# Expert outputs added by GpSimd for 32 of 64 row tiles, by VectorE for the rest; four buffers for the rows that feed layer 1's gates

## What is computed

```python
x  = L0_attn_x
xn = layernorm(x)
x  = x + L0_attn(xn) + L0_moe(xn)     # 16 heads of 8, attention between the heads of one row
xn = layernorm(x)
x  = x + L1_attn(xn) + L1_moe(xn)     # two gated causal convolutions over time

def moe(xn):                          # 8 experts, hidden size 512, two experts per row
    top_w, top_i = top2(xn @ W_gate)
    return sum(weight * (gelu(xn @ W_in[e] + b_in[e]) @ W_out[e] + b_out[e]) for the two experts e)
```

## Time and profile before

| | us |
|---|---|
| median of 3 runs | 1330.55 (1329.0 to 1339.67) |
| the profiled execution | 1335.22 |
| its span, first to last instruction | 1333.3 |
| busy: PE / DVE / ACT / POOL | 1042.1 / 739.9 / 583.7 / 803.9 |

### The profile page before, as it was taken

The page is one execution under the profiler, slowest core; times in us unless marked ns, Lnnn a source line. Parts: engine busy times, 40 slices in busy tenths (PEclk is TensorE's granted clock), DMA queues, the critical chain, the costliest instruction groups (busy, mean ns, idle before and its releaser), DMA issues. The chain is left out here.

```text
span 1333.3 us, 19064 instructions
## 1 busy us (share of the span) xinstructions
PE 1042.1 (78%) x6498; PEld 879.2 (66%) x6498; DVE 739.9 (55%) x953; ACT 583.7 (44%) x1518; POOL 803.9 (60%) x669
## 2 busy tenths in 40 slices
PE   5553776788988898888714678898879999999995
PEld 4521333367777777777613577888868888888884
DVE  7755988998888898888697643211122200000007
ACT  1200111166676777767503673000006666666651
POOL 4065675568888888888875136566544544444444
PEclk9876886799999999999856888998979999999998
DMA  9912322335554555555281021698966867666649
GB/s 294 355 47 102 120 84 109 108 93 151 155 162 139 154 170 149 161 150 159 68 325 57 1 84 44 197 279 252 296 196 195 270 193 196 194 190 196 199 135 356
DMA packets 120245, 226.03 MB, mean 170 GB/s; under 512 B 16961, under 2 KB 80405, under 8 KB 118102
## 3 DMA queue, kind: packets, MB, share of 16 engines
q1 hardware_dynamic: 102164, 188.45, 46.1%
q0 software_dynamic: 17600, 35.71, 7.3%
q10 hardware_dynamic: 386, 0.66, 0.2%
HBM read 157.33 MB, written 67.42 MB: 169 GB/s over the span
## 5 line engine op out<-in xcount | busy, mean ns | idle before, releaser
L498 POOL DMA_INDIRECT y_tok<-FF,yidx x284 | 283.3, 997 | 205.9 <-ACT FF L586 142.6
L490 POOL DMA_INDIRECT sorted_x<-XN,idx x256 | 247.9, 968 | 140.1 <-issue 88.0
L810 PE MATMUL ps<-FF 128*128 128x128 f32 x2272 | 285.8, 280 | 0.0
L810 PEld LDWEIGHTS ps<-FF 128*128 128x128 f32 x2272 | 274.0, 197 | 15.6 <-issue 4.8
L797 PE MATMUL ps<-FF 128*128 128x256 f32 x1136 | 272.3, 383 | 0.0
L576 ACT ACTIVATE FF<-ps,FF 128x256 f32<-128x256 f32 x568 | 231.4, 473 | 36.8 <-PE ps L797 29.1
L797 PEld LDWEIGHTS ps<-FF 128*128 128x128 f32 x1136 | 206.9, 192 | 22.7
L294 POOL TENSOR_TENSOR BG<-TPB 128x2048 f32<-128x2048 f32 x42 | 188.8, 4519 | 30.0 <-ACT TPB L603 20.8
L838 PE MATMUL ps<-BG,cst 128*128 128x512 f32 x176 | 105.4, 767 | 57.8 <-DVE BG L1144 40.5
L1176 DVE TENSOR_TENSOR BG<-ps,TPB 128x1024 f32<-128x1024 f32 x128 | 147.3, 1212 | 0.0
L1187 DVE TENSOR_REDUCE BG<-BG 128x256 f32<-128x4096 f32 x32 | 141.0, 4406 | 0.0
(11 more groups left out here) (203 smaller groups left out, 1462.0 us busy)
## 6 DMA issues: line engine op xcount, KB each, us to landing
FF<-in_moe SPq DMA_DIRECT2D x142, 514.0 KB
TPB<-in_kpad SPq DMA_DIRECT2D x22, 1024.0 KB
sorted_x<-TPB SPq DMA_DIRECT2D x36, 520.0 KB, 5.4
FF<-sorted_x SPq DMA_DIRECT2D x142, 130.0 KB
BG<-y_tok SPq DMA_DIRECT2D x12, 1024.0 KB, 9.2
FF<-in_kpad SPq DMA_DIRECT2D x10, 1024.0 KB
y_tok<-FF,yidx POOLq DMA_INDIRECT x284
xt_d<-BG SPq DMA_DIRECT2D x16, 256.0 KB, 4.4
```

The lines of the kernel that those rows point to most:

```text
L490: pool.indirect_dma_start(sorted_x[layer], bass.IndirectOffsetOnAxis(ap=idx[:, k, j:j + 1], axis=0), XN[:, j, :], None).then_inc(s_sc, 16)
L498: pool.indirect_dma_start(y_d[layer], bass.IndirectOffsetOnAxis(ap=yidx[:, G % 4, r:r + 1], axis=0), ys[:, G % 4, r * D:(r + 1) * D], None ...
L810: t = pe.matmul(psY[:, r * P:(r + 1) * P], hT[:, G % 2, m, r * P:(r + 1) * P], wc[:, G % 4, HID + m * D:HID + (m + 1) * D], start=False, s ...
```

## The change

Four things are altered. (1) Between the layers POOL adds only pieces 0 to 3 (`ADD_POOL = 4`), adding the two outputs to `X` one after the other; pieces 4 to 7 are added by DVE with the same two instructions inside rounds 2 and 3, ahead of their statistics. (2) POOL's `wait_ge(s_comb, 8)` ahead of its normalised rows goes. (3) The gate rows have four buffers, two of `xg` and two of `xT`, so that an engine waits for the transposes of four groups before instead of two; and DVE makes the rows of groups 1, 3, 5, 7, 11 and 15 only, ACT all others, so groups 9 and 13 move from DVE to ACT. (4) At the end DVE adds both outputs of all eight pieces, and POOL none.

```diff
-            def add_outputs(layer, i):
-                pool.wait_ge(s_yl[i], 16 * (layer + 1))
-                y = outputs(layer, i)
-                return pool.tensor_tensor(y[:, :, 0:D], y[:, :, 0:D], y[:, :, D:2 * D], ALU.add)
-
-            for i in range(8):
-                plink(add_outputs(0, i))
+            for i in range(ADD_POOL):
+                pool.wait_ge(s_yl[i], 16)
                 pool.wait_ge(s_xup, 4 * i + 4)
-                xv = X[:, 8 * i:8 * i + 8, :]
-                pool.tensor_tensor(xv, xv, outputs(0, i)[:, :, 0:D], ALU.add).then_inc(s_comb, 1)
-            pool.wait_ge(s_comb, 8)
+                y, xv = outputs(0, i), X[:, 8 * i:8 * i + 8, :]
+                plink(pool.tensor_tensor(xv, xv, y[:, :, D:2 * D], ALU.add))
+                pool.tensor_tensor(xv, xv, y[:, :, 0:D], ALU.add).then_inc(s_comb, 1)
...
-            for i in range(1, 7):
-                add_outputs(1, i).then_inc(s_ysum, 1)
...
+        def by_dve(g):
+            return g % 4 == 3 or g % 4 == 1 and g < NG // 2
+        def gate_rows(g):
+            return (xg, xT)[g % 2][:, (g // 2) % 2, :]
...
-                for g in (4 * q, 4 * q + 2):
-                    wait(act, s_tr, NG + g - 1 if g >= 2 else 0)
-                    for k in range(4):
-                        t = norm_rows(xg[:, 0, k * D:(k + 1) * D], 4 * g + k, 1)
-                    t.then_inc(s_hg[0], 1)
+                for g in range(4 * q, 4 * q + 4):
+                    if not by_dve(g):
+                        wait(act, s_tr, NG + g - 3 if g >= 4 else 0)
+                        for k in range(4):
+                            t = norm_rows(gate_rows(g)[:, k * D:(k + 1) * D], 4 * g + k, 1)
+                        t.then_inc(s_hg, 1)
...
-            def combine(i):
-                y = outputs(1, i)
-                rv = R[:, 8 * i:8 * i + 8, :]
-                if 1 <= i < 7:
-                    dve.wait_ge(s_ysum, i)
-                else:
-                    dve.wait_ge(s_yl[i], 32)
-                    link(dve.tensor_tensor(rv, rv, y[:, :, D:2 * D], ALU.add))
-                dve.tensor_tensor(rv, rv, y[:, :, 0:D], ALU.add).then_inc(s_comb, 1)
-                dve.wait_ge(s_comb, 8 + i + 1)
+            def combine(layer, dst, i):
+                dve.wait_ge(s_yl[i], 16 * (layer + 1))
+                y = outputs(layer, i)
+                dv = dst[:, 8 * i:8 * i + 8, :]
+                link(dve.tensor_tensor(dv, dv, y[:, :, D:2 * D], ALU.add))
+                dve.tensor_tensor(dv, dv, y[:, :, 0:D], ALU.add).then_inc(s_comb, 1)
+                dve.wait_ge(s_comb, 8 * layer + i + 1)
...
             for q in range(4):
-                dve.wait_ge(s_comb, 2 * q + 2)
+                for i in (2 * q, 2 * q + 1):
+                    if i < ADD_POOL:
+                        dve.wait_ge(s_comb, i + 1)
+                    else:
+                        combine(0, X, i)
                 stats_of(X, 16 * q, 16 * q + 16)
```

More of the change, by code:

```diff
@@ L52 @@
 ROWS_PARTS = 7
+ADD_POOL = 4
 COUNTS_AT = 7
@@ L246, in mixed_layers @@
         s_comb = sem("combined")
-        s_ysum = sem("expert_outputs_summed")
         s_resst = sem("x1_stored")
         s_resld = sem("x1_loaded")
-        s_hg = [sem(f"gate_rows{n}") for n in range(2)]
+        s_hg = sem("gate_rows_of_scalar")
+        s_hd = sem("gate_rows_of_vector")
         s_xnr = sem("layer1_rows_ready")
@@ L765, in transposes_and_gates @@
                         bank = psH[g % 4]
-                        pe.wait_ge(s_hg[g % 2], g // 2 + 1)
+                        made = len([n for n in range(g + 1) if by_dve(n) == by_dve(g)])
+                        pe.wait_ge(s_hd if by_dve(g) else s_hg, made)
                         wait(pe, s_xt, NG + g - 3 if g >= 4 else 0)
                     for k in range(4):
-                        src = XN[:, 4 * g + k, 0:D] if layer == 0 else xg[:, g % 2, k * D:(k + 1) * D]
+                        src = XN[:, 4 * g + k, 0:D] if layer == 0 else gate_rows(g)[:, k * D:(k + 1) * D]
                         t = pe.transpose(bank[:, k * P:(k + 1) * P], src, ident)
@@ L1265, in _ @@
                 for g in (4 * q + 1, 4 * q + 3):
-                    wait(dve, s_tr, NG + g - 1 if g >= 2 else 0)
-                    for j in range(4 * g, 4 * g + 4):
-                        t = dve.tensor_scalar(xg[:, 1, (j - 4 * g) * D:(j - 4 * g + 1) * D], X[:, j, :], rstd[:, 1, j:j + 1],
-                                              shift[:, 1, j:j + 1], ALU.mult, ALU.add)
-                    t.then_inc(s_hg[1], 1)
+                    if by_dve(g):
+                        wait(dve, s_tr, NG + g - 3 if g >= 4 else 0)
+                        for k in range(4):
+                            j = 4 * g + k
+                            t = dve.tensor_scalar(gate_rows(g)[:, k * D:(k + 1) * D], X[:, j, :], rstd[:, 1, j:j + 1],
+                                                  shift[:, 1, j:j + 1], ALU.mult, ALU.add)
+                        t.then_inc(s_hd, 1)
             ratio = best[:, 5, :]
@@ L1289, in _ @@
             dve.wait_ge(s_xnr, ROWS_PARTS)
-            for n in range(2):
-                dve.wait_ge(s_hg[n], NG // 2)
+            dve.wait_ge(s_tr, 2 * NG)
             dve.wait_ge(s_resst, 16 * 8)
@@ L1326, in _ @@
                 dve.wait_ge(s_oev, 2 * i + 2)
-                combine(i)
+                combine(1, R, i)
                 for g in (2 * i + 4, 2 * i + 5):
```

## The result

The changed kernel takes 1317.74 us (median of 20 runs, 1310.82 to 1324.09), the one before 1329.40 in 20 runs beside them (1321.49 to 1339.67): a ratio of 0.9912, 95% interval 0.9894 to 0.9931, or 11.7 us less (9.2 to 14.1). The forecast was 10.7 us less. The profiled execution took 1315.85 us, its span is 1314.0 us. Against the profiled execution of before (1335.22) that is 19.4 us, more than the medians show, so the first question is which part of the 19.4 belongs to the change.

A forecast was written before the change was run, and what follows sets the result against it. Between the layers all wait for DVE's first shift, its short products held by POOL's adds. Terms -11.8 + 2.4 - 0.5 - 0.8 = -10.7 us, from the median 1330.55 to 1320; range 1311 to 1329.

The forecast's parts named there:

- The stalls of round 0: Between the layers: without POOL's adds of pieces 4 to 7, DVE's first shift comes 11.8 us earlier.
- the other 1.5 us: DVE's product at 694.49, before round 0's statistics, would take 0.42 us without POOL beside it instead of 1.93.
- The rounds: Rounds 1 to 3 with DVE's adds: 8.9, 13.1, 12.0 and 2.0 contention, together 36.0 us, 2.4 more than before.
- the contention: Rounds 2 and 3: DVE's eight adds lose 2.0 us to POOL's normalised rows; bounds 0 and 3.4.
- Last shift to routing: Gate rows of groups 9 and 13 on ACT: routing begins 0.5 us sooner after the last shift; bounds 1.2 less, 1.0 more.
- The end: End of the kernel, DVE adding alone: pieces 3.73 us each, 27.4 us in all, 0.8 less; bounds 0 and 1.6 less.
- The first, over 1% faster: DVE's adds hardly meet POOL and ACT's square root is not late: 13.6 us less, 1317; chance 0.24.
- The second, a loss after 758 us: After routing, one more wait like ACT's 8.17 us takes the gain to 2.5 us: 1328; chance 0.08.
- The third, adds at 3.29 us: DVE's eight adds become the bound at 3.29 us each: 3.5 us slower, 1334; chance 0.04.
- The fourth, a round 1 of 10.8 us: Four buffers fail, ACT and PE keep round 1 at 10.8 us: 1322; chance within the forecast's 0.64.

The follow-up runs named there:

- e3: Kernel before, with POOL's adds of pieces 4 to 7 started only after the first shift; ratio 1.0011 to the kernel before.
- e1: Changed kernel, but POOL adds all eight pieces to `X` between the layers; ratio 0.9944 to the kernel before.
- e9: Changed kernel; POOL adds pieces 0 to 2, sums outputs of pieces 3 to 6 beside statistics, normalised rows after fourth shift; 1312.46 us.
- e5: Changed kernel; POOL sums the outputs of pieces 4 and 6 beside DVE's statistics, its normalised rows after the fourth shift; ratio 0.9894 to the kernel before.
- e7: Changed kernel, with POOL's normalised rows all started after the fourth shift; ratio 0.9888 to the kernel before.

## Why the prediction was right, and where a term was mis-sized

**The stalls of round 0 (-11.8).** Measured -11.45, and the short products at 0.17 us. The 10.3 us inside round 0 came out at 10.4 (16.64 to 6.25). The mis-sized part is the other 1.5 us, which did not show where the prediction put them: the product before the statistics took 1.93 us again, at 690.01, since DVE came to it 4.5 us earlier than in the trace that was read (694.49) while POOL's eighth add ended at about the same time (694.15; 693.85 before), so it ran beside piece 3 instead of piece 4. It took 1.93 to 1.95 in all seven profiles in which POOL makes these eight adds and then stops or waits. Another product gave 1.05 instead (2.04 at 682.43 before, 0.99 at 679.00 after). That is luck: the same product took 0.85 in e3, where POOL's adds up to there are those of the kernel before. In the trace of three pieces, where POOL was through in time, the product before the statistics took 0.42, as priced. The assumption that failed is that POOL's last kept add ends ahead of that product, as it did in the one trace that was read.

**The rounds (+2.4).** Measured +1.0 (34.60 against 33.59). Round 1, put at 8.9, took 8.77, and DVE's idle time of 1.07 for the square root was in it as predicted. For rounds 2 and 3 the instructions were put at 13.1 and 12.0, and without POOL beside them they took 13.06 and 12.03. The mis-sized term is the contention: "60% of 0.46 for eight adds is 2.2. I take 2.0" is 0.7 as measured. The 60% came from DVE's adds beside POOL's adds of 2.35 us, where DVE gives way; beside POOL's rows of 0.46 us POOL gave way, about 4 us in each round, and was not on the path. From the rule of the Trainium skill, SBUF — State Buffer, section Who interferes with whom, the prediction had worked out a saving of 9.3 us if each add stood behind a POOL instruction, 12.7 if none did; the stages show 11.9, and an add lost 0.09 us on average (0.37 / 4), so that nearly the whole waiting fell on POOL. The same section of the Trainium skill also says that the order of issue decides who waits. That fits better than a share of POOL's instruction did: of the four rows beside the adds of 709.37 to 713.32 three began 0.2 to 0.3 us after an add. The first began 0.04 us ahead of one (709.33) and waited all the same, so it is not the whole account.

**Last shift to routing (-0.5).** Measured -0.61. PE's clock bears on it, as the bounds allowed: the stage took 10.08 and 10.09 us in e1 and e9, where the granted clock was 1.00 all through it, 10.50 in the changed kernel, where it was 0.70 on average, and 12.11 in e5, with the last logits at 0.50 and 0.82.

**The end (-0.8).** Measured -0.88: 27.29 against 28.17 us, and 27.28 or 27.29 in all eight kernels in which DVE adds alone. But the 28.17 of before is no fixed number: with POOL's sums it was 28.17, 28.41 and 26.90 in three profiles. In the 28.17 four of DVE's adds were held, the two of the earlier trace rows and:

```profile
1317.73 3.06 DVE L1202 TENSOR_TENSOR BG<-BG 128x1024 f32<-128x1024 f32 x1
...
1322.03 2.60 DVE L1202 TENSOR_TENSOR BG<-BG 128x1024 f32<-128x1024 f32 x1
```

In the 26.90 (the moved adds alone) they were:

```profile
1304.61 3.29 DVE L1202 TENSOR_TENSOR BG<-BG 128x1024 f32<-128x1024 f32 x1 [1.00 <-POOL BG L519]
...
1309.14 2.06 DVE L1202 TENSOR_TENSOR BG<-BG 128x1024 f32<-128x1024 f32 x1
...
1312.43 2.07 DVE L1202 TENSOR_TENSOR BG<-BG 128x1024 f32<-128x1024 f32 x1
...
1315.74 1.22 DVE L1202 TENSOR_TENSOR BG<-BG 128x1024 f32<-128x1024 f32 x1
```

Here there is one add of 3.29 and two near 2.06, and then it was POOL's sum that waited (3.28 us from 1315.88, begun 0.14 us into the last add shown). So this part of the change gains up to 1.1 us or loses 0.4, by how the two engines fall against each other.

**The rivals.** The first, over 1% faster for want of contention, was nearly right in its premise for POOL's rows (0.7 us lost, not 2.0) and is refuted in its other half: the square root is late (1.07 us), and the change gives 11.9, not 13.6. The second, a loss after 758 us, is not seen; but the stretch from routing to the first add at the end varies by 12 us over the profiles of all kernels, which is wider than the single wait that was priced, and its cause was not tried. The third, adds at 3.29 us, fell: the worst took 1.36. The fourth, a round 1 of 10.8 us, fell with 8.77; it is what happens with two buffers (10.76).

**What was missed.** The prediction looked at what DVE's adds and POOL's rows do to each other, and not at DVE's gate rows beside POOL's long adds. The trace that it read had a sign of this, an instruction with one tensor as input that took 0.17 us in round 1 and ended here with POOL's add (705.75 to 708.11):

```profile
705.82 2.32 DVE L1013 TENSOR_SCALAR var<-rawv 128x16 f32<-128x16 f32 x1
```

It did no harm, since the change moves those adds away ahead of the gate rows, but it decides whether POOL could have kept them.

## What to carry to other kernels

When a 128x16 instruction shows 2 us in a trace, compare its end with the end of the other engine's instruction at that time; if they agree, move the long instruction to beside something that is shown not to be held, here the statistics, and not merely out of the stretch where it was seen to hurt. Before work is put on an engine, look at what stands ahead of it on that engine's list: with the same adds the rounds grew by 1.0 us where four buffers stood ahead of them and by 10.4 (43.95 against 33.59) where two did, of some 11 gained. And split two profiles into stages from an instruction that the change can't reach: of 19.4 us between these two, 7.4 lay in stages that the edits don't touch, and the medians bore that out.

## What the runs showed of the hardware that had not been expected

- An instruction of DVE with one tensor as input and a scale and a shift per row (128x128, fp32, 0.27 us) is held by POOL's adds as the two-input ones are: four took 9.61 and 8.24 us instead of 1.1, eight took 4.21 and 6.43 instead of 2.2. The Trainium skill, SBUF — State Buffer, section Who interferes with whom, counts such a scaling instruction among those that can use the shared ports; these rows agree. Beside POOL's own short rows the same instruction lost next to nothing (2.20 us for eight at 698.47, with POOL's rows from 698.54; 2.14 in e7, without them).
- The statistics instruction was not held in any profile: 3.17 to 3.20 us for sixteen, beside POOL's adds (e5, e9) and without.
- Who waits is not fixed by the engine. DVE's short products and single adds waited for POOL's adds of 2.35 us one by one; POOL's rows waited for DVE's adds (1.42 us each instead of 0.46). Where two single instructions met, the one that had clearly begun first ran undisturbed: POOL's sum at 1321.20 in the kernel before took 2.34 us and DVE's add of 1322.03 2.60 instead of 1.23; in e9 DVE's add at 709.16 took 1.22 us and POOL's sum of 709.33 3.27 instead of 2.35. What decides when both are ready was not settled.
